# Two-step range reduction and clamps ahead of the Sin activations, in a kernel on eight cores

## What is computed

```python
xn = layernorm(x)                                      # [4, 4096, 1024]
magnitude = sigmoid(xn @ W_mag.T + b_mag) * 5
phi = random_phases * position * 0.01
mem_r = cumsum(magnitude * xn * cos(phi)); mem_i = cumsum(magnitude * xn * sin(phi))
inv = 1 / sqrt(cumsum(magnitude) + 1e-8)
phi_q = phi + xn @ W_q.T + b_q
rr = inv * (mem_r * cos(phi_q) + mem_i * sin(phi_q))
ri = inv * (mem_i * cos(phi_q) - mem_r * sin(phi_q))
context = [xn*cos(phi), xn*sin(phi), rr, ri]           # 4096 wide, layernormed
attn = xn + gelu(ln(context) @ W1.T + b1) @ W2.T + b2
ffn = (gelu(gelu((silu(xn@w1.T*s1) * (xn@w2.T*s2)) @ h1.T*h1s) @ h2.T*h2s) @ w3.T) * s3
out = x + attn + ffn
```

## Time and profile before

| what | us |
|---|---|
| runs shown, median of 2 | 5094.95 |
| the two runs | 4981.43 and 5208.47 |
| the profiled execution, its own time | 4863.24 |
| its span, slowest core (core 0) | 4861.7 |
| spans of the 8 cores | 4813.3 to 4861.7 |
| TensorE busy in the span | 3546.9 (73%) |
| VectorE busy in the span | 1546.8 (32%) |
| ScalarE busy in the span | 894.2 (18%) |
| POOL busy in the span | 399.1 (8%) |

### The profile page before, as it was taken

How to read it: one execution, slowest core, us unless ns; L and a number is a source line. 1 busy time by engine, 2 the same in 40 slices (tenths; PEclk the granted TensorE clock), 3 DMA queues, 4 the chain that set the end, 5 groups by cost and what they waited for, 6 DMA issues and landing times.

```text
span 4861.7 us, 45746 instructions; the slowest of 8 cores (4813.3 to 4861.7 us)
## 1 busy us (share of the span) xinstructions
PE 3546.9 (73%) x15210; PEld 1540.5 (32%) x15504; DVE 1546.8 (32%) x3659; ACT 894.2 (18%) x1201; POOL 399.1 (8%) x756
## 2 busy tenths in 40 slices
PE   3235102128869999888699988787999887899993
PEld 3211001003324443333244433333444333344441
DVE  2451688740134440521244306112442060100003
ACT  2111102210113331001133220012332200110100
POOL 0001101000110000002100000021000000200000
PEclk9997556559989998899899989998999799999997
DMA  2126999986764443577644435675444276844443
GB/s 75 41 57 124 110 117 113 110 104 121 115 118 147 148 155 113 104 133 116 117 149 152 151 103 112 135 123 126 154 150 152 81 140 115 124 143 156 147 148 74
DMA packets 123392, 592.46 MB, mean 122 GB/s; under 512 B 15611, under 2 KB 15644, under 8 KB 76060
## 3 DMA queue, kind: packets, MB, share of 16 engines
q0 software_dynamic: 108288, 545.31, 53.6%
q1 hardware_dynamic: 14876, 44.21, 2.8%
HBM read 857.90 MB, written 75.50 MB: 192 GB/s over the span
## 4 chain that ended last, share of the span: by engine, by line
PE 58%; DMA 19%; DVE 12%; issue 7%; another core or an unknown queue 2%; ACT 1%; DVEq 1%; SPq 0%; POOLq 0%; ACTq 0%; POOL 0%
PE ps L508 47%; DMA wstage<-w_t 10%; DMA wstage<-fw_t 5%; PE ps L1109 2%; PE ps L1118 2%; DMA wstage<-wmag_t 2%; PE ps L835 2%; PE ps L1014 1%; PE ps L1004 1%; DMA xo<-x_fm 1%; DVE big L586 1%; PE ps L333 1%; PE ps L398 1%; DVE xo L582 1%
## 5 line engine op out<-in xcount | busy, mean ns | idle before, releaser
L508 PE MATMUL ps<-big,wstage 128*128 128x512 bf16 x11790 | 2699.2, 388 | 395.7 <-DMA wstage<-w_t 164.9
L508 PEld LDWEIGHTS ps<-big,wstage 128*128 128x128 bf16 x12032 | 1183.5, 99 | 1915.0 <-issue 590.1
L1128 DVE SCALAR_TENSOR_TENSOR big<-ps,svv_s,big 128x512 bf16<-128x512 f32 x128 | 96.1, 751 | 959.3 <-PE ps L1118 959.3
L835 PE MATMUL ps<-xn_hi,wstage 128*128 128x512 bf16 x504 | 125.7, 413 | 324.2 <-DVE big L708 222.7
L1109 PE MATMUL ps<-xn_hi,wstage 128*128 128x512 bf16 x1002 | 240.7, 379 | 36.2 <-DMA wstage<-fw_t 29.5
L1118 PE MATMUL ps<-xn_hi,wstage 128*128 128x512 bf16 x1002 | 240.3, 380 | 31.6 <-DMA wstage<-fw_t 26.1
L330 DVE COPY big<-ps 33x128 f32<-33x128 f32 (+1 forms) x36 | 11.8, 327 | 614.3 <-PE ps L1014 525.2
L1170 ACT ACTIVATE big<-ps,svv_h2s 128x512 bf16<-128x512 f32 x128 | 87.9, 687 | 620.7 <-PE ps L508 620.4
L1014 PE MATMUL ps<-big,sel_b_sb 128*33 128x512 bf16 x128 | 72.9, 570 | 173.3 <-ACT big L1010 144.9
L1192 DVE SCALAR_TENSOR_TENSOR obuf<-ps,svv_s,obuf 128x512 f32<-128x512 f32 x32 | 24.0, 751 | 548.1 <-PE ps L508 548.1
L228 POOL DMA_DIRECT2D wstage<-w_t x128 | 67.7, 529 | 1446.1 <-PE ps L508 1397.0
(11 more groups left out here) (158 smaller groups left out, 2408.1 us busy)
## 6 DMA issues: line engine op xcount, KB each, us to landing
wstage<-h1b POOLq DMA_DIRECT2D x128, 1024.0 KB, 5.1
wstage<-h2b POOLq DMA_DIRECT2D x128, 1024.0 KB, 5.1
wstage<-w_t POOLq DMA_DIRECT2D x96, 1024.0 KB, 9.0
wstage<-fw_t POOLq DMA_DIRECT2D x256, 256.0 KB, 5.0
h1b<-h_t POOLq DMA_DIRECT2D x32, 1024.0 KB, 69.0
h2b<-h_t POOLq DMA_DIRECT2D x32, 1024.0 KB, 164.0
xo<-x_fm SPq DMA_DIRECT2D x48, 512.0 KB, 5.4
wstage<-w_t POOLq DMA_DIRECT2D x32, 512.0 KB, 5.2
```

The lines of the kernel that those rows point to most:

```text
L508: last = e.matmul(psum[bank][:, 0:NMOV], wt_ap, mov_fn(k), start=(k == 0), stop=(k == K - 1))
L835: last = e.matmul(psum[bank][:, 0:NMOV], wt_ap, mov_xn(k), start=(k == 0), stop=(k == KD - 1))
L1128: V(lambda e, m=m, bankB=bankB, yb=yb, ctxb=ctxb: e.scalar_tensor_tensor(out=big2[:, yb + m * M:yb + (m + 1) * M], in0=psum[bankB][:, 0:NM ...
```

## The change

The whole turn that is added or taken off is no longer one constant, 2*pi, but two, CW1 = 6.28125 and CW2, the rest, so that it is done in two instructions, and each argument is clamped before its Sin: to plus or minus 3.1415925 ahead of the sine, and to the range from -4.7123885 to 1.5707962 ahead of the cosine (whose activation adds pi/2). Per call of `emit_sincos` that is four more VectorE instructions: two `scalar_tensor_tensor` of 128 x 512 f32 and two `tensor_scalar` with two constants (min, then max), 13 in place of 9. Each set of phases in `emit_rot_scalars` gets the same four on 128 x 8. The results change in their last digits.

```diff
+PI_CL = float(np.float32(3.1415925))
+COS_HI = float(np.float32(1.5707962))
+COS_LO = float(np.float32(-4.7123885))
...
         V(lambda e: e.scalar_tensor_tensor(out=sf(q, A), in0=sf(q, C),
-                                           scalar=TWO_PI_F, in1=sf(q, B),
+                                           scalar=CW1, in1=sf(q, B),
                                            op0=ALU.mult, op1=ALU.add),
           reads=sfb(q, C) + sfb(q, B), writes=sfb(q, A))
+        V(lambda e: e.scalar_tensor_tensor(out=sf(q, B), in0=sf(q, C),
+                                           scalar=CW2, in1=sf(q, A),
+                                           op0=ALU.mult, op1=ALU.add),
+          reads=sfb(q, C) + sfb(q, A), writes=sfb(q, B))
+        V(lambda e: e.tensor_scalar(out=sf(q, A), in0=sf(q, B), scalar1=PI_CL,
+                                    scalar2=-PI_CL, op0=ALU.min, op1=ALU.max),
+          reads=sfb(q, B), writes=sfb(q, A))
         S(lambda e: e.activation(out=tf(sin_t), in_=sf(q, A), func=AF.Sin),
           reads=sfb(q, A), writes=[tfb(sin_t)])
         V(lambda e: e.tensor_scalar(out=sf(q, C), in0=sf(q, A), scalar1=PI_F / 2,
                                     scalar2=None, op0=ALU.is_gt),
           reads=sfb(q, A), writes=sfb(q, C))
         V(lambda e: e.scalar_tensor_tensor(out=sf(q, B), in0=sf(q, C),
-                                           scalar=-TWO_PI_F, in1=sf(q, A),
+                                           scalar=-CW1, in1=sf(q, A),
                                            op0=ALU.mult, op1=ALU.add),
           reads=sfb(q, C) + sfb(q, A), writes=sfb(q, B))
+        V(lambda e: e.scalar_tensor_tensor(out=sf(q, A), in0=sf(q, C),
+                                           scalar=-CW2, in1=sf(q, B),
+                                           op0=ALU.mult, op1=ALU.add),
+          reads=sfb(q, C) + sfb(q, B), writes=sfb(q, A))
+        V(lambda e: e.tensor_scalar(out=sf(q, B), in0=sf(q, A), scalar1=COS_HI,
+                                    scalar2=COS_LO, op0=ALU.min, op1=ALU.max),
+          reads=sfb(q, A), writes=sfb(q, B))
         S(lambda e: e.activation(out=tf(cos_t), in_=sf(q, B), func=AF.Sin,
...
# and the same four on s8(...) in emit_rot_scalars
```

More of the change, by code:

```diff
@@ L658, in emit_rot_scalars @@
             V(lambda e: e.scalar_tensor_tensor(out=s8(3), in0=s8(5),
-                                               scalar=TWO_PI_F, in1=s8(4),
+                                               scalar=CW1, in1=s8(4),
                                                op0=ALU.mult, op1=ALU.add),
               reads=s8b(5) + s8b(4), writes=s8b(3))
+            V(lambda e: e.scalar_tensor_tensor(out=s8(4), in0=s8(5),
+                                               scalar=CW2, in1=s8(3),
+                                               op0=ALU.mult, op1=ALU.add),
+              reads=s8b(5) + s8b(3), writes=s8b(4))
+            V(lambda e: e.tensor_scalar(out=s8(3), in0=s8(4), scalar1=PI_CL,
+                                        scalar2=-PI_CL, op0=ALU.min,
+                                        op1=ALU.max),
+              reads=s8b(4), writes=s8b(3))
             S(lambda e, jx=jx: e.activation(
@@ L669, in emit_rot_scalars @@
             V(lambda e: e.scalar_tensor_tensor(out=s8(4), in0=s8(5),
-                                               scalar=-TWO_PI_F, in1=s8(3),
+                                               scalar=-CW1, in1=s8(3),
                                                op0=ALU.mult, op1=ALU.add),
               reads=s8b(5) + s8b(3), writes=s8b(4))
+            V(lambda e: e.scalar_tensor_tensor(out=s8(3), in0=s8(5),
+                                               scalar=-CW2, in1=s8(4),
+                                               op0=ALU.mult, op1=ALU.add),
+              reads=s8b(5) + s8b(4), writes=s8b(3))
+            V(lambda e: e.tensor_scalar(out=s8(4), in0=s8(3), scalar1=COS_HI,
+                                        scalar2=COS_LO, op0=ALU.min,
+                                        op1=ALU.max),
+              reads=s8b(3), writes=s8b(4))
             S(lambda e, jx=jx: e.activation(
```

## The result

Over 12 executions of the changed kernel and 10 of the kernel before, side by side, the medians are 4949.90 and 4951.19 us, and the ratio is **1.0099 (95% interval 1.0053 to 1.0144)**: about 1% slower, within 2%. The best execution of before took 4851.96 us, the best of the changed kernel 4882.79. The profiled execution took 4898.61 us against 4863.24.

The account below looks back on a forecast made before the run. Bound taken: prologue VectorE beside DMA conversions of h1 and h2, the later deciding W1's start. VectorE's 69.5 us less 34.1 slack gives 35.5, plus 1.7 clock: 37.2; 4863.24 to 4900.4 profiled, 5132 as median, range 4890 to 5250.

Parts of the forecast that it names:

- the base of the absolute number: Whole kernel: median 5094.95 of before's two runs (4981.43 and 5208.47), plus 37 us, giving 5132 us.
- the likeliest case: The forecast itself: VectorE's longer prologue course passes the slack before W1; 37.2 us, 0.8% more; chance 0.74.
- VectorE's course: VectorE's work through the prologue to block 31: 3.0 + 21.3 + 42.6 + 2.6 = 69.5 us later, at 1124.0.
- The slack: At the start of W1: VectorE's block 31 done 34.1 us before TensorE's second 16 matmuls, which wait for both courses.
- The clock: At W1's second 16 matmuls: after a second idle stretch they run at the low clock, 5.4 against 3.63, 1.7 us.
- The 48 calls: Calls of emit_sincos beside h1 and h2: 128 us more on VectorE, none of it charged.
- Core 0 stays the slowest: Across the cores: core 0 at 4900.4 us, core 7 at 4892.6 after the change.
- The other course still ends last: Rival, prologue: the DMA conversion of h1 and h2 still decides, nothing added, 4863 us; chance 0.04.
- The full price: Rival, prologue: conversions end later too, so the whole 69.5 us reaches TensorE, 4933 us; chance 0.06.
- Dependent waits are free: Rival, added VectorE steps: VectorE only 49 us later, TensorE's second half 15 us later, 4878 us; chance 0.04.
- The clamps starve the load queue: Rival, h1 and h2: each clamp holds up a load by 0.43, 41 us in all, 4941 us; chance 0.02.
- The hidden calls aren't hidden: Rival, h1 and h2: evictions fall behind, the 48 calls reach the path, 128 + 37 = 165 us, 5028; chance 0.07.

Follow-up runs that it names:

- e6_nowait: Changed kernel with L471 writing another scratch tile, so it needn't wait for Sin; VectorE's prologue course 604.8 us against 607.1, first W1 eviction 1126.2, no ratio.
- e3_lite: Changed kernel with the added steps kept only in emit_rot_scalars and emit_lite(0); course 561.0 us, first W1 eviction 1086.9 (before 1088.8); its span isn't used.
- e4_mid0: Changed kernel with the added steps kept only in emit_mid(0); course 583.1 us, first W1 eviction 1100.5, mean span 4851.0 (before 4841.4), no ratio.
- e5_more: Changed kernel with each clamp done three times in the 24 prologue calls, old steps in the 48 others; first W1 eviction 1177.1, mean span 4921.8 us.
- e7: Kernel before with the last 4 of 32 h2 conversions moved, in 32 pieces, behind h1's weight loads in pass 0; first W1 eviction 1054.1, ratio 0.9955.
- e8: Changed kernel with the last 4 of 32 h2 conversions moved, in 32 pieces, behind h1's weight loads in pass 0; first W1 eviction 1124.5, no ratio.
- e2_hidden: Changed kernel with the added steps only in the 48 calls beside h1 and h2, none in the prologue; ratio to before 0.9977 (0.9938 to 1.0016).
- e9_abs: Changed kernel with the cosine as Sin(pi/2 - |A|), one VectorE instruction replacing four; course 559.1 us, ratio to before 1.0007.
- The |A| form: Cosine as Sin(pi/2 - |A|): in the changed kernel ratio 1.0007; in the kernel before, with 5 h2 conversions moved beside h1, ratio 0.9908 (both to before).

## Why the prediction was right and wrong

**What was wrong: the base of the absolute number.** The step "their median at 5094.95; I add the same 37 us and predict 5132" failed. That median was of two executions, 2.4% and 7.1% above the profiled one; ten executions of before have a median of 4951.19, and the three further sets of 13, 13 and 23 have 4866.76, 4869.34 and 4864.05. So the base was 144 us too high even against the ten. The step's other half, that the 37 us would show between two such medians, failed as well: they differ by 1.29 us, the other way. The changed kernel's median is 4949.90, 182 us below 5132, inside the range of 4890 to 5250, which had been made wide for that scatter. The profiled execution's own forecast, 4900.4, met 4898.61. A base far from the profiled execution had to be distrusted: the page's span is what the sum was made of. "About 2% is what a measurement of this kernel tells from no change" was too coarse: the interval of the ratio is 0.5% to either side, and leaves out 1.

**The effect.** 37.2 us, 0.8%, were forecast; the ratio says 1.0%, with 0.5 to 1.4% in its interval; the profiles say 35.7 at W1 and 32 in the mean span, and the mean spans of more executions 33 to 38. This was the likeliest case, and within 2%.

- *VectorE's course.* 69.5 forecast, 69.0 measured: 23.6 up to the start of `emit_mid(0)` (3.0 + 21.3 forecast) and 45.4 from there (42.6 + 2.6). The price of 2.66 a call held; `e6_nowait` puts the wait for Sin at 2.3 (2.6 forecast).
- *The slack.* 34.1 us were read on core 0. `e3_lite` (22.9 us, none arrives), `e4_mid0` (45.0, 11.7 arrive) and `e5_more` (52.5 more, 52.6 arrive) fit one slack of about 35 us, and `e7` with `e8` name its owner. It is a mean: in the kernel before, the first W1 matmul starts between 25.0 (core 4) and 33.0 us (core 1) behind block 31, and the second 16 follow some 5 us later. The earlier trace rows is read one block too early: its first row is block 14's, and block 15 was done at 1028.06. That moves only the start of the first 16 matmuls, and nothing hangs on it. The label "another core or an unknown queue" was read rightly.
- *The clock.* 1.7 us for the second 16 matmuls at the 1.2 GHz level were forecast: 5.4 in place of 3.63. On core 5 they took 4.97, on core 0 6.48 (0.405 each), where the granted clock was 0.50 until 1116 and 0.69 from there to 1119. The price of 0.335 each was read from a stretch in which the clock had already risen (0.50 from 1083 to 1086, 0.88 from 1086 to 1089), so that the low clock's own price is higher.
- *The 48 calls.* Not charged, and `e2_hidden` shows that they cost at most 8 us, and nothing that can be seen. The lock between VectorE and ScalarE came as described (434 us of waiting), and no h1 or h2 got longer.
- *VectorE's busy time.* 161 us more forecast, 159.4 measured.
- *Core 0 stays the slowest.* Wrong: it was the fastest in the changed kernel's profile, with a span of 4857.7 us, 4.0 shorter than its own before, where the sum had 37 longer. The step took core 0's own start of the course as given. It began at 516.1 before and at 503.8 after, for a reason ahead of the change. That the slowest core of one profile was about where the sum put it is partly luck; the means over the cores carry the claim.

**The rivals.** "The other course still ends last" is true of `e3_lite` and `e9_abs`, not of the change. "The full price" is false at W1 of the changed kernel and true past the slack (`e5_more`); its footing, that L708 released `emit_A1(0)`, was the trace's guess. The row after, which answers to the earlier trace rows, has the same wait with another name:

```profile
727.52 16.25 PE L868 MATMUL ps<-xn_hi,wstage 128*128 128x512 bf16 x63 [225.82 <-DVE big L770]
```

Over the eight cores `emit_A1(0)` starts at 733.8 on the mean, before at 735.0, although VectorE's list up to there had grown: by 23.6 us to the start of `emit_mid(0)`. In `e5_more`, where that had grown by 41.7, it starts at 731.5. So it doesn't wait for VectorE, whichever line of it the trace names. "Dependent waits are free" gave 49 us of course; 69.0 were measured. The Trainium skill (VectorE: DVE Perf Modes, section The DRAIN you can't avoid) would have them free; here the trace decides against it. "The clamps starve the load queue" would have shown in `e2_hidden`, where 96 clamps more stand beside h1's and h2's loads; nothing shows (at most 8 us, for 41 in the rival's sum), and the loads of h1 land in 5.1 us as in the earlier trace rows. The stall that the Trainium skill (SBUF — State Buffer, section SBUF: two separate sides) describes, a DMA of GpSimd's queue whose descriptors wait for VectorE, is shown by no run here. "The hidden calls aren't hidden" fell with the same run.

## What to carry to other kernels

Where two courses end at one wait, find who holds the slack and how much: added work is free up to it and costs its full length beyond, so that harmless halves add up to a dear whole. A wait that the trace can't name ("an unknown queue", "issue"), or names after an engine that was done long before (L1066 in `e4_mid0`), is most cheaply named by shortening the suspect alone, and then again in the kernel where the other course should decide. Take a time's base from as many executions as there are, and be careful with a median of two.

## What was not expected of the hardware

- **The start of VectorE's course jumps.** The first Sin of `emit_rot_scalars` starts between 502.6 and 522.2 us in these two profiles, mostly near 504 or near 516, on one core or its neighbour, and not the same ones each time (before: 516.1, 503.9, 503.3, 515.6, 516.0, 502.6, 509.9, 522.2 on cores 0 to 7; changed: 503.8, 517.3, 516.2, 503.4, 510.0, 519.6, 514.9, 503.2). Core by core, the last block came between 50 and 86 us later in the changed kernel, for a course that was 68.5 to 69.6 longer on each. What lies ahead of it are weight loads among conversions; why it is 504 or 516 was not tried.
- **W1's own length wanders.** From first to last eviction W1 of pass 0 took 130.2 us before, 127.6 changed, 127.7 in `e4_mid0`, 128.8 in `e5_more` and 130.5 in `e8_move_after`, which starts W1 at the same time as the changed kernel and has the same matmuls; over all profiles it is 126.0 to 130.5, and doesn't follow the delay at its start. In all of them groups wait for their weights. The mean span wanders as well: 4829.0 to 4858.6 in the executions of before that the ratios use. So that 35.7 us at the start of W1 are 32 in the mean span of one pair of profiles needs no cause of its own.
- **The |A| form saved more than its steps.** 12.7 us were worked out for 24 calls against the kernel before, and 15.2 were measured; against the changed kernel 47 and 48.0. Where the other 2.5 us come from wasn't looked into.
